# A gated recurrence of 512 steps: the state's kept and fresh terms in separate matmuls, TensorE's turns written out

## The reference

```python
def step(h, inp):
    x_t, prop = inp
    comb = jnp.concatenate([x_t, h], axis=-1)
    z = jax.nn.sigmoid(comb @ Wz + bz)
    r = jax.nn.sigmoid(comb @ Wr + br)
    comb2 = jnp.concatenate([x_t, r * h], axis=-1)
    h_cand = jnp.tanh(comb2 @ Wh + bh)
    h_new = (1.0 - z) * h + z * h_cand
    h_next = jnp.where(prop, jnp.tanh(h_new @ Wp + bp), h_new)
    return (h_next, h_new)
```

## Time and profile before

| | us |
|---|---|
| median of 3 runs | 3470.85 |
| lowest and highest | 3466.49, 3475.07 |
| the profiled execution | 3473.07 |
| its span | 3471.3 |
| TensorE busy | 2859.3 (82%) |
| VectorE busy | 1350.2 (39%) |
| ScalarE busy | 850.5 (25%) |

### The profile page before, as it was taken

How to read it: one execution, slowest core, us unless ns; L and a number is a source line. 1 busy time by engine, 2 the same in 40 slices (tenths; PEclk the granted TensorE clock), 3 DMA queues, 4 the chain that set the end, 5 groups by cost and what they waited for, 6 DMA issues and landing times.

```text
span 3471.3 us, 74601 instructions
## 1 busy us (share of the span) xinstructions
PE 2859.3 (82%) x27890; PEld 2110.8 (61%) x27890; DVE 1350.2 (39%) x6286; ACT 850.5 (25%) x2694; POOL 432.5 (12%) x515
## 2 busy tenths in 40 slices
PE   7888787888888877539999995888965998999888
PEld 5666666666666666228888883335841343387467
DVE  5555555555555555201111113532333356511442
ACT  1222222222222222112222221123521121322332
POOL 0000000000000000340000004242143000000343
PEclk6555555555555555669999997999987899899989
DMA  5000000000000000136666662212434431000123
GB/s 190 2 2 2 2 2 2 2 2 2 2 2 2 2 2 2 42 124 197 196 196 194 194 188 79 91 67 91 127 98 136 89 73 24 0 0 0 38 76 106
DMA packets 182184, 230.14 MB, mean 66 GB/s; under 512 B 57496, under 2 KB 146176, under 8 KB 181440
## 3 DMA queue, kind: packets, MB, share of 16 engines
q1 hardware_dynamic: 159712, 162.01, 16.3%
q0 software_dynamic: 22240, 64.51, 5.6%
HBM read 166.32 MB, written 60.16 MB: 65 GB/s over the span
## 4 chain that ended last, share of the span: by engine, by line
issue 46%; PE 44%; DVE 3%; another core or an unknown queue 2%; DMA 1%; POOL 1%; SPq 1%; ACT 1%; DVEq 0%; ACTq 0%; POOLq 0%
PE bank L1573 8%; PE bank L1585 8%; PE bank L1771 5%; PE bank L1530 3%; PE bank L1519 3%; PE bank L1631 3%; PE bank L1699 2%; PE bank L1688 2%; PE bank L1872 2%; PE bank L1884 2%; PE bank L1640 2%; PE bank L1733 1%; PE bank L1560 1%; PE bank L1806 1%
## 5 line engine op out<-in xcount | busy, mean ns | idle before, releaser
L1435 PE MATMUL bank<-hpart,WB 128*128 128x8 f16 x13824 | 522.9, 170 | 183.2 <-DVE hpart L940 96.9
L1435 PEld LDWEIGHTS bank<-hpart,WB 128*128 128x128 f16 x13824 | 466.7, 105 | 326.0 <-DVE hpart L940 239.0
L1435 PE MATMUL bank<-rhpart,WB 128*128 128x8 f16 x6144 | 288.4, 171 | 84.8 <-DVE rhpart L924 84.8
L1435 PEld LDWEIGHTS bank<-rhpart,WB 128*128 128x128 f16 x6144 | 242.7, 106 | 130.6 <-DVE rhpart L924 128.1
L1573 PE MATMUL bank<-WA,WB 128*128 128x256 f32 x1248 | 309.2, 381 | 7.8 <-DMA WA<-in_L_ffn_b 7.8
L1585 PE MATMUL bank<-WB,hid 128*128 128x256 f32 x1248 | 313.8, 379 | 0.0
L1419 PE MATMUL bank<-XT,WB 128*128 (+1 forms) x792 | 305.1, 482 | 1.0
L1573 PEld LDWEIGHTS bank<-WA,WB 128*128 128x128 f32 x1248 | 238.1, 191 | 40.9 <-issue 8.2
L1585 PEld LDWEIGHTS bank<-WB,hid 128*128 128x128 f32 x1248 | 234.2, 190 | 30.3
L1031 DVE COPY WA<-bank 128x512 f32<-128x512 f32 x76 | 52.6, 692 | 511.6 <-PE bank L1560 511.6
L682 ACT ACTIVATE hid<-bank,b_up 128x256 f32<-128x256 f32 x312 | 148.1, 475 | 394.2 <-PE bank L1573 394.2
(11 more groups left out here) (314 smaller groups left out, 3822.2 us busy)
## 6 DMA issues: line engine op xcount, KB each, us to landing
WB<-in_L_ffn_w SPq DMA_DIRECT2D x78, 1024.0 KB, 7.7
WA<-tile_rows SPq DMA_DIRECT2D x86, 256.0 KB
expert_rows<-WA POOLq DMA_DIRECT2D x86, 256.0 KB, 2.7
GB<-gates SPq DMA_DIRECT2D x8, 2048.0 KB
tile_rows<-WA SPq DMA_DIRECT2D x4, 2496.0 KB, 17.3
WA<-in_L_ffn_b SPq DMA_DIRECT2D x40, 128.0 KB, 7.3
GB<-in_x SPq DMA_DIRECT2D x8, 512.0 KB, 7.4
out<-HT SPq DMA_DIRECT2D x16, 256.0 KB
```

Source lines behind the costliest of these rows:

```text
L1435: last = nc.tensor.matmul(bank[:, m * width + s * B:m * width + (s + 1) * B], wpart[:, g, w, k, m * P:(m + 1) * P], part[:, a, k * B:(k + ...
```

## The change

VectorE no longer forms `upd` and then the new state in the ring. It makes `gain` = (1 + tanh z) / 2 x scale early, the kept term `kept` = keep x h in full precision and in two f16 halves `kept_part`, and, when the candidate is there, the fresh term `fresh` = gain x cand, likewise with `fresh_part`. The new state is their sum, made afterwards.

TensorE sums the reset gate of steps 1 to 3 of a chunk from `kept_part` and `fresh_part`, 12 matmuls each, and the proposal in the same way. The kept one's matmuls stand after the candidate's matmuls of the step before and ahead of the piece of projection. The update gate of these steps still reads `hpart`, with waits of its own. `hpart` isn't made at a chunk's end, where `split_entry` writes it. TensorE's 32 turns are written out in place of the loop over pairs. The other edits let `ident`'s clearing and the norm's root use semaphores that exist already.

```diff
-                    nc.vector.tensor_tensor(keep_h[:], keep[:], h, ALU.mult)
+                    nc.vector.tensor_scalar(gain[:], gate_z[:], 0.5 * HSCALE, 0.5 * HSCALE, ALU.mult, ALU.add)
                     dve.wait_ge(keep_ready, n + 1)
+                    nc.vector.tensor_tensor(kept_part[:, 0], keep[:], h, ALU.mult).then_inc(k_part, 1)
+                    nc.vector.tensor_tensor(kept[:], keep[:], h, ALU.mult).then_inc(k_full, 1)
                     if s % (STEPS // 2) == 0:
                         dve.wait_ge(hist_copied, it * 2 + 1 + s // (STEPS // 2))
+                    dve.wait_ge(k_full, n + 1)
+                    nc.vector.tensor_tensor(kept_part[:, 1], kept[:], kept_part[:, 0], ALU.subtract).then_inc(k_part, 1)
                     dve.wait_ge(c_ready, n + 1)
-                    nc.vector.scalar_tensor_tensor(upd[:], gate_z[:], 1.0, cand[:], ALU.add, ALU.mult).then_inc(upd_ready, 1)
-                    dve.wait_ge(upd_ready, n + 1)
-                    nc.vector.scalar_tensor_tensor(hpart[:, 0], upd[:], 0.5 * HSCALE, keep_h[:], ALU.mult, ALU.add).then_inc(h_part, 1)
-                    nc.vector.scalar_tensor_tensor(hist[:, s], upd[:], 0.5 * HSCALE, keep_h[:], ALU.mult, ALU.add).then_inc(h_full, 1)
-                    dve.wait_ge(h_full, n + 1)
-                    nc.vector.tensor_tensor(hpart[:, 1], hist[:, s], hpart[:, 0], ALU.subtract).then_inc(h_part, 1)
+                    nc.vector.tensor_tensor(fresh_part[:, 0], gain[:], cand[:], ALU.mult).then_inc(u_part, 1)
+                    nc.vector.tensor_tensor(fresh[:], gain[:], cand[:], ALU.mult).then_inc(u_full, 1)
+                    dve.wait_ge(u_full, n + 1)
+                    nc.vector.tensor_tensor(fresh_part[:, 1], fresh[:], fresh_part[:, 0], ALU.subtract).then_inc(u_part, 1)
+                    if (s + 1) % CHUNK:
+                        nc.vector.tensor_tensor(hpart[:, 0], kept[:], fresh[:], ALU.add).then_inc(h_part, 1)
+                    nc.vector.tensor_tensor(hist[:, s], kept[:], fresh[:], ALU.add).then_inc(h_full, 1)
+                    if (s + 1) % CHUNK:
+                        dve.wait_ge(h_full, n + 1)
+                        nc.vector.tensor_tensor(hpart[:, 1], hist[:, s], hpart[:, 0], ALU.subtract).then_inc(h_part, 1)
...
-                        wait = lambda a: pe.wait_ge(e_part, (it * NP + s // CHUNK) * 2 + a + 1)
+                        recur(gates[0], 0, W, s, hpart, lambda a: pe.wait_ge(e_part, (it * NP + s // CHUNK) * 2 + a + 1)).then_inc(r_psum, 1)
+                        recur(gates[1], 1, W, s, hpart, None).then_inc(z_psum, 1)
                     else:
-                        wait = lambda a: pe.wait_ge(h_part, (n - 1) * 2 + a + 1)
-                    recur(gates[0], 0, W, s, hpart, wait).then_inc(r_psum, 1)
-                    recur(gates[1], 1, W, s, hpart, None).then_inc(z_psum, 1)
+                        recur(gates[0], 0, W, s, fresh_part, lambda a: pe.wait_ge(u_part, (n - 1) * 2 + a + 1)).then_inc(r_psum, 1)
+                        recur(gates[1], 1, W, s, hpart,
+                              lambda a: pe.wait_ge(h_part, (it * NP * 3 + s // CHUNK * 3 + s % CHUNK - 1) * 2 + a + 1)).then_inc(z_psum, 1)
                     recur(gates[2], 2, W, s, rhpart, lambda a: pe.wait_ge(rh_part, n * 2 + a + 1)).then_inc(c_psum, 1)
-                    next(following, None)
-                    if (s + 1) % CHUNK == 0:
-                        recur(gates[3], 3, NP * B, s // CHUNK, hpart,
-                              lambda a: pe.wait_ge(h_part, n * 2 + a + 1)).then_inc(p_psum, 1)
+                    from_kept = lambda a: pe.wait_ge(k_part, n * 2 + a + 1)
+                    if (s + 1) % CHUNK:
+                        recur(gates[0], 0, W, s + 1, kept_part, from_kept)
+                        next(following, None)
+                    else:
+                        recur(gates[3], 3, NP * B, s // CHUNK, kept_part, from_kept)
+                        next(following, None)
+                        recur(gates[3], 3, NP * B, s // CHUNK, fresh_part,
+                              lambda a: pe.wait_ge(u_part, n * 2 + a + 1)).then_inc(p_psum, 1)
                         next(following, None)
...
-            with pe.Fori(0, TURNS // 2) as it2:
-                for turn in range(2):
-                    gru_turn(it2 * 2 + turn, banks[turn * 4:turn * 4 + 4], banks[4 - turn * 4:8 - turn * 4])
+            for it in range(TURNS):
+                a = it % 2 * 4
+                gru_turn(it, banks[a:a + 4], banks[4 - a:8 - a])
```

More of the change, by code:

```diff
@@ L214, in build_program @@
         keep = sb("keep", [P, KD * B])
-        keep_h = sb("keep_h", [P, KD * B])
-        upd = sb("upd", [P, KD * B])
+        gain = sb("gain", [P, KD * B])
+        kept = sb("kept", [P, KD * B])
+        fresh = sb("fresh", [P, KD * B])
+        kept_part = sb("kept_part", [P, 2, KD * B], F16)
+        fresh_part = sb("fresh_part", [P, 2, KD * B], F16)
         const_ready = sem("const_ready")
-        ident_zero = sem("ident_zero")
         x_loaded = [sem(f"x_loaded{i}") for i in range(B // 2)]
@@ L234, in build_program @@
         e_part, e_full = sem("e_part"), sem("e_full")
-        keep_ready, upd_ready = sem("keep_ready"), sem("upd_ready")
+        keep_ready, k_full, k_part = sem("keep_ready"), sem("k_full"), sem("k_part")
+        u_full, u_part = sem("u_full"), sem("u_part")
         hist_copied = sem("hist_copied")
@@ L279, in build_program @@
         cent_sum, cent_root, cent_ready = sem("cent_sum"), sem("cent_root"), sem("cent_ready")
-        norm_sum, norm_root = sem("norm_sum"), sem("norm_root")
         silu_half = sem("silu_half")
@@ L498, in _ @@
             nc.gpsimd.memset(part_row[0:1, 1:2], 0.0).then_inc(row_made, 1)
-            nc.gpsimd.memset(ident[:], 0.0).then_inc(ident_zero, 1)
+            nc.gpsimd.memset(ident[:], 0.0).then_inc(row_made, 1)
             nc.gpsimd.memset(ones[:], 1.0).then_inc(const_ready, 1)
@@ L511, in _ @@
             nc.gpsimd.memset(rsq[:, :, RL - 1:RL], 1.0).then_inc(prefer_ready, 1)
-            pool.wait_ge(ident_zero, 1)
+            pool.wait_ge(row_made, 5)
             nc.gpsimd.affine_select(out=ident[:], in_=ident[:], compare_op=ALU.not_equal, fill=1.0, base=0,
@@ L785, in _ @@
             routing_copies(2, 2 * NTILE, square)
-            act.wait_ge(norm_sum, 1)
-            nc.scalar.activation(r_y, r_x, ACT.Sqrt).then_inc(norm_root, 1)
             act.wait_ge(exp_in, 2)
+            nc.scalar.activation(r_y, r_x, ACT.Sqrt).then_inc(exp_done, 1)
+            act.wait_ge(exp_in, 3)
             nc.scalar.activation(r_eq, r_sel, ACT.Exp).then_inc(exp_done, 1)
@@ L1168, in _ @@
             take_logits(2, r_raw, RL)
-            V.tensor_copy(r_x, r_raw[:, :, RL - 1:RL]).then_inc(norm_sum, 1)
-            dve.wait_ge(norm_root, 1)
+            V.tensor_copy(r_x, r_raw[:, :, RL - 1:RL]).then_inc(exp_in, 1)
+            dve.wait_ge(exp_done, 2)
             link(V.tensor_scalar(r_z, r_y, 1e-12, None, ALU.max))
@@ L1177, in _ @@
             V.tensor_tensor(r_sel, r_log, wide(r_m1), ALU.subtract).then_inc(exp_in, 1)
-            dve.wait_ge(exp_done, 2)
+            dve.wait_ge(exp_done, 3)
             link(V.tensor_tensor(r_tmp, r_eq, r_mask1, ALU.mult))
```

## The result

| | before | after |
|---|---|---|
| median, us | 3470.85 (5 runs, 3466.49 to 3480.81) | 3500.0 (5 runs, 3492.6 to 3509.59) |
| profiled execution, us | 3473.07 | 3497.23 |
| its span, us | 3471.3 | 3495.5 |
| recurrence, first to last proposal, us | 1354.9 | 1382.2 |

The ratio to the kernel before is 1.008 (95% interval 1.0055 to 1.0106), so the change made the kernel slower by 0.8%. Forecast were 3505 us and slower. The kernel before has two runs more here than in the table ahead of the prediction, taken beside the changed one; its median is the same.

A forecast was written before the change was run, and what follows sets the result against it. The prediction took the recurrence, a closed ring through TensorE, ScalarE and VectorE at 2.32 us a step, as the bound. Late pieces and the shorter ring, +78 us, less 45.5 for jumps, gave +32.5: 3505 us, range 3462 to 3554.

The forecast's parts named there:

- the ring: Recurrence step as a closed chain through TensorE, ScalarE and VectorE, 2.32 us; one vector operation less gains 0.21 a step.
- Turns written out: TensorE's loop over pairs of turns: 15 jumps of 3.0 us each go, all on the path, gain 45.5 us.
- rival D: Straight code shows its fetches as the jumps did: 45.5 us given back, 3551 us; chance 7%.
- The update gate costed at nothing: In three steps of a chunk the update gate ends some 0.07 us later, covered by `keep`'s spare time: no cost.
- The kept matmuls: 12 more matmuls in every step, starting at 1.63 and through at 2.05 us; alone they would fit before 2.09.
- What is queued behind: Projection piece after the kept matmuls makes the fresh group late: net 0.49 us with f32, 0.15 with a bias sum.
- The 0.09 that a late group gets back: A late TensorE group finds both halves ready and loses its inner wait: tanh at 0.51 instead of 0.60 us.
- The lone row: Profile row of a single f32 projection matmul in the recurrence, read as holding TensorE at most 0.62 us.
- A, the clock: Rival: the fuller recurrence is granted TensorE's upper clock level, 3380 us or less; chance 6%.
- B, pieces at their lower bound: Rival: projection pieces cost least, 0.58 us for f32 and 0.14 for a bias sum, giving 3466 us; chance 16%.
- C, VectorE's loop: Rival: VectorE's longer loop is fetched again at 31 jumps, 2.8 less 0.8 us each, giving 3567 us; chance 5%.
- waits of 0.2 for `kept_part` in every step: Expected sign in the profile: TensorE waits 0.2 us for the kept term's halves in every recurrence step.

The follow-up runs named there:

- x6_no_kept: Changed kernel without the kept term's matmuls on TensorE, every vector instruction kept: 3311.47 us, 0.9548 of the kernel before.
- x1_turns_only: Kernel before with only TensorE's 32 turns written out: 3421.35 us, 0.9875 of the kernel before.
- x4_no_f32: Changed kernel without the projection's f32 matmuls in all turns but the first: 3343.74 us, 0.965 of the kernel before.
- x8_even: Changed kernel, projection piece ahead of the kept matmuls, f32 matmuls in all four places behind a proposal: 3356.78 us, 0.9685 of the kernel before.
- x3_piece_first: Changed kernel with the projection's piece moved ahead of the kept term's matmuls: 3371.88 us, 0.9726 of the kernel before.

## Why the prediction was right, step by step

*What bounds the recurrence.* The ring and its six stations were read correctly: in x6_no_kept, where nothing covers it, each step is 2.10, the 2.32 less the 0.21 of one vector operation.

*Turns written out.* 45.5 us forecast, 44.7 measured by x1_turns_only. That straight code would show its own gaps (rival D) is refuted: the list of TensorE's waits there has no entry named issue within the recurrence. The Trainium skill, "Runtime: NRT & Kernel Launch", section "Instruction fetch mechanics", says that a taken branch out of the held window waits until its target is fetched. It gives no time for it; the traces agree, with 3.0 us for a jump.

*The update gate costed at nothing.* Right, by `keep` at 1.20 in x6_no_kept.

*The kept matmuls.* They start 1.63 after the group (701.28 to 702.91) and the piece follows at 2.04 (703.32); the prediction had 1.63 and 2.05. Alone they would fit: x4_no_f32.

*What is queued behind.* The f32 piece holds TensorE for 0.59 (703.32 to 703.91), the value of the back-to-back row, not the 0.62 that I took. The lone row had given only a bound, as the group after it was waiting for VectorE just as long. A step is 2.57 instead of 2.60, or 2.27 instead of 2.26 with a bias sum; a turn 43.50 instead of 43.68. The 0.09 that a late group gets back falls elsewhere than the prediction's steps had it: a chunk's first step starts from a group that isn't late and takes 2.63 (701.28 to 703.91), and the proposal's late group takes 0.97 (700.31 to 701.28) instead of 1.05. Over a chunk the count is the same.

*The sum.* Ring: 16 x 32 x 0.21 = -108 forecast, -110 from 41.24 to 37.80 a turn. Kept matmuls and pieces: 32 x (10 x 0.49 + 6 x 0.15) = +186 forecast, 32 x (43.50 - 37.80) = +182 measured. Jumps: -45.5, -44.7. In all +32.5 forecast, +27.3 between the proposals. The medians say +29, but their ratio's interval allows 19 to 37 us, so the terms are confirmed by the times between proposals and not by the median.

*The rivals.* A, the clock: it is 0.50 over the recurrence, with TensorE's matmuls busy 1274 of 1394 us. The Trainium skill, "TensorE: Matmul & The Clock Gate", table "Why this matters for your kernels", advises keeping TensorE busy for the upper level; this fuller queue didn't get it. B, pieces at their lower bound: right for the f32 piece (0.59), wrong for the bias sum, which held TensorE 0.22 (705.96 to 706.18) and started late besides. C, VectorE's loop: every turn holds one of its jumps, so equal turns don't decide it, but distances inside a turn do. From proposal to proposal the kernel after takes 11.00, 11.10, 10.62 and, over the jump, 10.78. The last two have as many pieces of each kind, so the jump costs at most 0.16 of C's 2.0. In x8_even, where every chunk has the same load, it is 9.83 with and without the jump.

*One sign was misjudged.* I expected waits of 0.2 for `kept_part` in every step. The matmul rows show nearly none, because the candidate's last matmul is modelled to last 0.17 and covers the gap; it stands in the weight loads instead, 64.0 us before 512 groups, 0.125 each.

## What to carry to other kernels

A hole in one engine's queue is a place in time: work that fits it must also be ordered so that it runs while the hole is open. An instruction that waits, put ahead of free filler, leaves the hole's beginning empty and pushes the filler onto the ring. Before adding work to such a hole, add up everything that is to stand in it: here 0.86 us less the 0.21 by which the ring was to shrink was 0.65, for 0.42 and 0.59. If the sum is over, put first what needs to wait for nothing.

## What the runs showed of the hardware

Cutting a matmul's moving columns didn't cut its time in proportion: with f32 weights of 128 x 128, 128 columns held TensorE 0.59 us at the lower clock and 64 columns 0.47. From these two, 0.12 belong to 64 columns and some 0.35 to what doesn't depend on them, an estimate from the two rows; that this is the loading of the weights is possible, but not shown.

A sustained queue didn't raise the clock: in x3_piece_first, too, whose busy times for the recurrence follow, the granted share is 0.50.

```profile
48.00:1311.00 1263.00, 1164.47 (x26892) 1050.10 (x26890) 910.63 (x7234) 303.33 (x1648) 29.00 (x63) 0.50 0.02 5
```
